# The expert blocks' down product as three fp32r products of split operands, with the weight's low part made on GpSimd

## What is computed

```python
shared = jax.nn.silu(flat @ sg) * (flat @ su) @ sd
probs = jax.nn.softmax(flat @ router_w, axis=-1)
topk_p, topk_i = jax.lax.top_k(probs, K_TOP)            # K_TOP = 2, 8 experts
topk_p = topk_p / (jnp.sum(topk_p, axis=-1, keepdims=True) + 1e-09)
cw = jnp.zeros((N, E)).at[jnp.arange(N)[:, None], topk_i].add(topk_p)
h = jax.nn.silu(jnp.einsum('nd,edf->nef', flat, wg)) * jnp.einsum('nd,edf->nef', flat, wu)
eo = jnp.einsum('nef,efd->ned', h, wd)
routed = jnp.einsum('ned,ne->nd', eo, cw)
return (shared + routed).reshape(B, T, D)
```

## Time and profile before

| | |
|---|---|
| three runs | 1410.91 us median, 1410.36 to 1414.53 |
| the profiled execution | 1408.87 us, its span 1407.1 us |
| TensorE busy | 97% of the span |
| VectorE, ScalarE, GpSimd busy | 61%, 56%, 59% of the span |
| granted TensorE clock | 1.00 throughout |
| expert blocks, gate product 0 to 14 | 1245.03 to 1381.54 us |

### The profile page before, as it was taken

The page is one execution under the profiler, slowest core; times in us unless marked ns, Lnnn a source line. Parts: engine busy times, 40 slices in busy tenths (PEclk is TensorE's granted clock), DMA queues, the critical chain, the costliest instruction groups (busy, mean ns, idle before and its releaser), DMA issues. The chain is left out here.

```text
span 1407.1 us, 23293 instructions
## 1 busy us (share of the span) xinstructions
PE 1371.2 (97%) x8766; PEld 1121.1 (80%) x8766; DVE 853.3 (61%) x1424; ACT 794.8 (56%) x1235; POOL 833.8 (59%) x721
## 2 busy tenths in 40 slices
PE   5999999999999999999999999999999899989998
PEld 3678888888888888888888888888888567766664
DVE  5565565566556556665655666565555657657564
ACT  3455666666566666656666665666655613245652
POOL 3466777777677777767777776777766434210002
PEclk9999999999999999999999999999999999999999
DMA  7577666766766676766666766766687645279994
GB/s 283 168 121 138 108 126 107 133 118 132 127 123 123 110 132 115 132 128 125 108 126 116 130 116 137 133 107 119 101 178 140 159 151 215 82 302 364 365 366 136
DMA packets 115231, 218.10 MB, mean 155 GB/s; under 512 B 13360, under 2 KB 49200, under 8 KB 108976
## 3 DMA queue, kind: packets, MB, share of 16 engines
q1 hardware_dynamic: 111968, 209.00, 66.2%
q0 software_dynamic: 1280, 4.20, 0.9%
q10 hardware_dynamic: 1872, 3.41, 0.6%
HBM read 132.67 MB, written 16.78 MB: 106 GB/s over the span
## 5 line engine op out<-in xcount | busy, mean ns | idle before, releaser
L587 POOL TENSOR_TENSOR p_parts<-probs,p_parts 128x512 fp32r<-128x512 f32 x256 | 340.2, 1348 | 248.5 <-ACT p_parts L644 248.5
L644 ACT ACTIVATE p_parts<-probs 128x512 fp32r<-128x512 f32 x256 | 147.7, 625 | 237.8 <-PE banks L962 237.8
L769 DVE TENSOR_TENSOR probs<-banks,probs 128x1024 f32<-128x1024 f32 x128 | 156.7, 1224 | 145.7 <-ACT probs L650 145.7
L674 ACT ACTIVATE probs<-probs 128x1024 f32<-128x1024 f32 x128 | 135.9, 1062 | 140.0 <-POOL probs L594 139.9
L911 PE MATMUL banks<-wv_hi,x_hi 128*128 128x512 f32 x512 | 206.7, 404 | 0.0
L929 PE MATMUL banks<-x_hi,wk_hi 128*128 128x512 f32 x512 | 201.7, 394 | 0.0
L912 PE MATMUL banks<-wv_lo,x_hi 128*128 128x512 f32 x512 | 201.1, 393 | 0.0
L913 PE MATMUL banks<-wv_hi,x_lo 128*128 128x512 f32 x512 | 200.1, 391 | 0.0
L931 PE MATMUL banks<-x_hi,wk_lo 128*128 128x512 f32 x512 | 199.6, 390 | 0.0
L930 PE MATMUL banks<-x_lo,wk_hi 128*128 128x512 f32 x512 | 199.3, 389 | 0.0
L958 PE MATMUL banks<-p_parts,v_hi 128*65 128x128 f32 x1024 | 191.7, 224 | 0.0
(11 more groups left out here) (305 smaller groups left out, 2679.5 us busy)
## 6 DMA issues: line engine op xcount, KB each, us to landing
queries<-q_scratch SPq DMA_DIRECT2D x256, 128.0 KB, 6.5
keys<-wo_room SPq DMA_DIRECT2D x128, 256.0 KB, 5.6
keys<-turned_odd SPq DMA_DIRECT2D x128, 256.0 KB, 5.6
row_room<-in_ctx SPq DMA_DIRECT2D x64, 256.0 KB, 6.4
wo_room<-in_down SPq DMA_DIRECT2D x10, 1024.0 KB, 9.1
late_room<-in_gate SPq DMA_DIRECT2D x8, 1024.0 KB, 8.1
gate_raw<-in_up SPq DMA_DIRECT2D x8, 1024.0 KB, 7.2
up_raw<-in_gate SPq DMA_DIRECT2D x7, 1024.0 KB, 7.9
```

The costliest lines, as they stand in the source:

```text
L587: nc.gpsimd.tensor_tensor(p_parts[:, 1, j, :], probs[:, pair % 2, j, :], p_parts[:, 0, j, :].bitcast(F32), ALU.subtract).then_inc(p_lo_rea ...
L769: nc.vector.tensor_tensor(mine, ps_s[:, :, :, 0, :].rearrange("p j i n -> p (j i) n"), mine, ALU.add).then_inc(s_taken, 1)
```

## The change

- The down product becomes `product` on split operands: 12 fp32r matmuls. Its operands are `ht_hi` (ScalarE, in the place of `ht`), `ht_lo` (VectorE, `hidden_low`), `down_hi` (ScalarE, `down_high(j)` behind silu j) and `down_lo` (GpSimd, a subtraction of 128x2048 behind the scatters, one a block).
- The split down weights lie in the buffers of the shared expert's operands, xt_hi, xt_lo, h_hi and h_lo, so the gathers now land in raw[1] and raw[2].
- A down buffer is free when its low part is made, no longer after its product. Down loads 1 and 2 are issued in `mix`'s last stretch, behind a wait for its out products.
- `rank_tokens` comes ahead of up product 1 of the shared expert, not in its middle; `find_places` comes ahead of the first `h_lo`; `split_low(2)` behind `find_owners`.
- The transposes of rows 0 stand in front of the last quarter of the shared down product, and VectorE takes the low part of rows 0 ahead of the shared additions. The transposes of hidden 0 come behind gate product 1, not between its matmuls.
- `late_shares` is one batch in each of blocks 3 to 6, and the shares are transposed and copied in block 8, not 5.
- VectorE counts its steps with one semaphore in all stages.

```diff
@@ run_sp
                 if j >= 3:
-                    sp.wait_ge(e_down_done, j - 2)
+                    sp.wait_ge(down_lo_ready, j - 2)
                 sp.dma_start(down[j % 3], d["down"][expert]).then_inc(down_landed[j % 3], 16)
...
             load_unit(unit_of(0, UP), 1)
             load_unit(unit_of(1, GATE), 2)
+            sp.wait_ge(keep["out_done"], BATCH)
+            load_down(1, 2)
+            load_down(2, 3)
             load_unit(unit_of(1, UP), 2)
             sp.wait_ge(scattered, 16 * 2 * BATCH)
...
             load_rows(2)
-            load_down(1, 2)
             load_unit(unit_of(2, UP), 3)
@@ run_pool
                     nc.gpsimd.indirect_dma_start(d["row_scratch"], bass.IndirectOffsetOnAxis(pos[:, k, b:b + 1], 0),
                                                  x_norm[:, b, :], None).then_inc(scattered, 16)
+            for m in range(BLOCKS):
+                pool.wait_ge(down_hi_ready, m + 1)
+                nc.gpsimd.tensor_tensor(down_lo[m % 2], down[m % 3], down_hi[m % 2].bitcast(F32), ALU.subtract).then_inc(down_lo_ready, 1)
             for i in range(2):
                 pool.wait_ge(e_stored[i], 16 * ((BLOCKS - LATE + 1 - i) // 2))
@@ run_act
+            def down_high(m):
+                act.wait_ge(down_landed[m % 3], 16 * (m // 3 + 1))
+                if m == 0:
+                    act.wait_ge(gate_up_done, KT)
+                elif m == 1:
+                    act.wait_ge(shared_done, BATCH)
+                else:
+                    act.wait_ge(e_down_done, m - 1)
+                nc.scalar.activation(down_hi[m % 2], down[m % 3], ACT.Copy).then_inc(down_hi_ready, 1)
...
-                    nc.scalar.activation(ht[:, (j - 1) % 2], ps_turn, ACT.Copy).then_inc(ht_ready, 1)
+                    nc.scalar.activation(ht_hi[:, (j - 1) % 2], ps_turn, ACT.Copy).then_inc(ht_hi_ready, 1)
...
                     nc.scalar.activation(silu[:, j % 2, :], ps_gate[:, 0, :], ACT.Silu).then_inc(e_silu_ready, 1)
+                    down_high(j)
@@ run_dve
+            def hidden_low(m):
+                dve.wait_ge(ht_hi_ready, m + 1)
+                if m >= 2:
+                    dve.wait_ge(e_down_done, m - 1)
+                nc.vector.tensor_tensor(ht_lo[:, m % 2], ps_turn, ht_hi[:, m % 2].bitcast(F32), ALU.subtract).then_inc(ht_lo_ready, 1)
...
             choose()
-            split_low(2)
             for f in range(KT):
...
+                if f == 0:
+                    find_places()
                 dve.wait_ge(h_hi_ready, f + 1)
...
                 if f == 0:
-                    find_places()
                     find_owners()
+                    split_low(2)
...
             split_low(4)
+            rows_low(0)
             for b in range(BATCH):
                 dve.wait_ge(shared_done, b + 1)
                 nc.vector.tensor_tensor(y[:, b, :], ps_y[:, b, :], x3[:, b, :], ALU.add).then_inc(y_added, 1)
-            rows_low(0)
...
                 if j == 0:
                     rows_low(1)
+                else:
+                    hidden_low(j - 1)
...
-                if j == 3:
-                    late_shares()
+                if 3 <= j < 3 + BATCH:
+                    late_shares(j - 3)
+            hidden_low(BLOCKS - 1)
@@ run_pe
-            gate_or_up(1, UP, whole, range(KT // 2))
             rank_tokens()
-            gate_or_up(1, UP, whole, range(KT // 2, KT)).then_inc(gate_up_done, 1)
+            gate_or_up(1, UP, whole, range(KT)).then_inc(gate_up_done, 1)
...
                 pe.wait_ge(h_lo_ready, t + 1)
+                if t == KT - 1:
+                    pe.wait_ge(rows_landed[0], 16)
+                    for i in range(KT):
+                        tr = turn(ps_rows, rows[:, 0, :], i)
+                    tr.then_inc(rows_turned, 1)
...
+                if j == 1:
+                    pe.wait_ge(e_hidden_ready, 1)
+                    for t in range(KT):
+                        tr = turn(ps_turn, hidden[:, 0, :], t)
...
-                    pe.wait_ge(ht_ready, m + 1)
-                    pe.wait_ge(down_landed[m % 3], 16 * (m // 3 + 1))
+                    pe.wait_ge(ht_lo_ready, m + 1)
+                    pe.wait_ge(down_lo_ready, m + 1)
...
-                        mm = nc.tensor.matmul(ps_y[:, m % 2, :], ht[:, m % 2, t, :], down[m % 3][:, t, :],
-                                              start=(t == 0), stop=(t == KT - 1))
+                        mm = product(ps_y[:, m % 2, :], (ht_hi[:, m % 2, t, :], ht_lo[:, m % 2, t, :]),
+                                     (down_hi[m % 2][:, t, :], down_lo[m % 2][:, t, :]), t == 0, t == KT - 1)
```

More of the change, by code:

```diff
@@ L201, in prepare @@
         ones_ready = sem("a_ones_ready")
-        dve_step = sem("a_dve_step")
+        dve_step = keep["dve_step"]
         var_ready = sem("a_var_ready")
@@ L301, in run_dve @@
         def run_dve(dve):
-            chain = [0]
+            chain = keep["dve_steps"]
             def link(ins):
@@ L1103, in mix @@
         attn_turned, attn_t_ready, wo_done = (keep[n] for n in ("attn_turned", "attn_t_ready", "wo_done"))
-        dve_step = sem("c_dve_step")
+        dve_step = keep["dve_step"]
         var_ready = sem("c_var_ready")
@@ L1119, in mix @@
         out_done = sem("c_out_done")
+        keep["out_done"] = out_done
         out_t_ready = sem("c_out_t_ready")
@@ L1420, in experts @@
         rt_lo = sb("rt_lo", [P, 2, KT, P], F32R)
-        ht = sb("ht", [P, 2, KT, P])
+        ht_hi = sb("ht_hi", [P, 2, KT, P], F32R)
+        ht_lo = sb("ht_lo", [P, 2, KT, P], F32R)
+        down_hi, down_lo = [xt_hi[:], h_hi], [xt_lo[:], h_lo]
         by_token = x_norm[:, 0:2, :].rearrange("p a (b n) -> p (a b) n", n=LATE * P)
@@ L1456, in experts @@
         ps_logits = ps_y[:, 3, 0:BATCH * EXPERTS].rearrange("p (b e) -> p b e", e=EXPERTS)
-        gathered = [h_hi.bitcast(F32), h_lo.bitcast(F32)]
+        gathered = [raw[1], raw[2]]
         raw_landed, split_hi, split_lo = keep["split_landed"], keep["split_hi"], keep["split_lo"]
@@ L1469, in experts @@
         route_counted = sem("route_counted")
-        router_step = sem("router_step")
+        dve_step = keep["dve_step"]
         pos_ready = sem("pos_ready")
@@ L1482, in experts @@
         h_turned = sem("h_turned")
-        ht_ready = sem("ht_ready")
+        ht_hi_ready = sem("ht_hi_ready")
+        ht_lo_ready = sem("ht_lo_ready")
+        down_hi_ready = sem("down_hi_ready")
+        down_lo_ready = sem("down_lo_ready")
         e_down_done = sem("e_down_done")
@@ L1540, in run_sp @@
                     load_unit(unit_of(j, UP), expert_of[j])
-                load_down(j - 1, expert_of[j - 1])
+                if j > 3:
+                    load_down(j - 1, expert_of[j - 1])
             for b in range(BATCH):
@@ L1625, in run_dve @@
         def run_dve(dve):
-            chain = [0]
+            chain = keep["dve_steps"]
             def link(ins):
                 chain[0] += 1
-                ins.then_inc(router_step, 1)
-                dve.wait_ge(router_step, chain[0])
+                ins.then_inc(dve_step, 1)
+                dve.wait_ge(dve_step, chain[0])
             def per_token(a):
@@ L1869, in take_late @@
                         mm.then_inc(late_done, 1)
-            pe.wait_ge(rows_landed[0], 16)
-            for t in range(KT):
-                tr = turn(ps_rows, rows[:, 0, :], t)
-            tr.then_inc(rows_turned, 1)
             for j in range(BLOCKS + 1):
@@ L1882, in run_pe @@
                     pe.wait_ge(split_lo, v + 1)
[L1883 removed]
+                if j >= 2:
                     pe.wait_ge(e_hidden_ready, j)
[L1885 to L1886 removed]
+                    pe.wait_ge(ht_lo_ready, j - 1)
                 for t in range(KT):
@@ L1915, in run_pe @@
                     m = j - 1
-                    if j == 5:
+                    if j == 8:
                         turn_shares()
@@ L1963, in program @@
         keep["attn_t"] = room
+        keep["dve_step"], keep["dve_steps"] = sem("dve_step"), [0]
         keep["angles_landed"] = [sem(f"angles_landed{i}") for i in range(2)]
```

31 lines of the change are left out of this document (14 added, 17 removed).

## The result

The changed kernel took 1413.73 us (median of 20 runs, 1409.76 to 1416.98), the kernel before 1409.61 beside it (20 runs, 1407.79 to 1415.06). The ratio is 1.0019 with a 95% interval of 1.0010 to 1.0028, so 2.7 us more (1.4 to 3.9). The two medians by themselves lie 4.1 us apart; I go by the ratio, which has the interval. The prediction was 1413.3 us, and +2.4 for the change.

The account below looks back on a forecast made before the run. It took TensorE's matmuls to set the pace in the blocks. Start -2.2, gate 0 to 2 +1.6, gate 2 to 14 -2.4 and tail +5.4 sum to +2.4 us: 1413.3 from the median 1410.91, range 1406 to 1419.

Parts of the forecast that it names:

- GpSimd's subtraction: In each expert block, GpSimd's 128x2048 subtraction for the down weight's low part takes 4.5 us.
- The two engines keep each other out: In the blocks, VectorE's two-operand split of the up weight stands until GpSimd's subtraction finishes, showing 3.4 to 4.5 us.
- Rival B: In the blocks, the engines hardly block each other, so waits of 7.7 us go: 1405.6 us; chance 0.15.
- A wait in every second block: At the up product, the low weight comes 0.8 us late in every second block, 0.4 a block.
- down 2.4: From gate product 2 to gate product 14, the stretch falls from 119.7 to 117.3 us.
- Share blocks: In blocks 3 to 6, VectorE's share work makes ht_lo late: 0.8 us each, 0.4 more in block 3, 3.6 in all.
- Gate 0 to 2: From gate product 0 to 2, TensorE waits 0.5 and 2.3 us, so the stretch grows 1.6 to 18.4.
- The start: Before gate product 0, earlier places and scatters bring it forward 2.2 us, with a 0.3 wait for the rows.
- The tail: After gate product 14, the gathers queue behind GpSimd's fifteenth subtraction: 31.0 us for 25.6, up 5.4.
- rival C: After gate product 14, the gathers don't set the end; tail 24.3 to 27 us, total 1407 to 1409; chance 0.07.
- Rival D: In the blocks, transfers need 9.56 us against 9.2 and the slack doesn't hold: 1415 to 1416 us; chance 0.06.
- Rival A: In the blocks, GpSimd's subtraction takes 5.4 us, mean wait 0.85 a block and more: 1420 us; chance 0.22.

Follow-up runs that it names:

- e3: Changed kernel with each GpSimd subtraction of 128x2048 cut into four of 128x512; 1413.17 us, ratio 1.0018 to the kernel before.
- e5: Changed kernel with GpSimd computing only the first two down low parts, which later blocks reuse; 1399.46 us, ratio 0.9922 to the kernel before.
- e6: Changed kernel with the share work spread over blocks 1 to 12, its transposes in block 13; 1412.95 us, ratio 1.0018 to the kernel before.
- e4: Changed kernel with the old order of the start; 1415.91 us, ratio 1.0034 to the kernel before.
- e10: Kernel before the change with only the new order of the start; 1409.14 us, ratio 0.9984 to the kernel before.
- e1: Changed kernel with the fifteenth down weight's low part on VectorE instead of GpSimd; 1405.91 us, ratio 0.9966 to the kernel before.
- e9: Changed kernel, all down low parts on VectorE ahead of the up split, one small share operation in each of blocks 0 to 13; 1397.39 us, ratio 0.9914.
- e12: Changed kernel with GpSimd computing the first quarter of each down low part once more; 1428.53 us, ratio 1.0127 to the kernel before.
- e11: Changed kernel with the down loads of blocks 1 and 2 at their old queue places; 1412.07 us, ratio 1.0009 to the kernel before.

## Why the prediction was right, point by point

The mechanisms were right: the two engines that keep each other out, the waits at the places named, and the queue in the tail. That the sum of the stages hit so closely (+2.33 for +2.4) is luck: the start gave 0.7 us more than worked out and the blocks 0.8 less, and these cancelled. So is part of the match in the total: 1413.3 was added up from a median of 1410.91 for the kernel before, which then measured 1409.61.

- **The down product** (2.85, measured 2.88; a block without waits 9.2, measured 9.23): right. The 0.03 in twelve blocks is 0.4 us.
- **GpSimd's subtraction** (4.5): 4.63. The line through its 512 and 1024 rows was the right estimate, the average of the attention stage the wrong one.
- **The two engines keep each other out:** shown by e3 and e5. Rival B is out, although its price was about right between gate 2 and gate 14: without its 2.3 for block 1 its 7.7 us leave 5.4 there, and e5 gained 6.1.
- **A wait in every second block** (0.8): 0.90, of which the rows give 0.62 as idle; three of them add 0.3 us. With the transposes at 1.04 for 0.95 and the 0.4 above, this is the 0.8 by which "down 2.4" missed (-1.62).
- **Share blocks** (3.6): the four intervals from gate 4 to gate 8 exceed 9.23 by 3.57. The size was right, its naming was in part not: by e6 1.9 of it stand there without the share work too, and moving this work away nets only 1 us.
- **Gate 0 to 2** (+1.6): +1.63, with waits of 0.46 and 2.14 for the 0.5 and 2.3 predicted.
- **The start** (-2.2): -2.88, the largest miss. The eight scatters took 12.3 us from the first's start to the last's end, for 13.3 before (two of them, issued while splits of VectorE's ran, took 2.00 and 2.17 us for the usual 0.96; before, 2.71 and 1.89), so the wait of 0.3 for the rows did not come, and gate 0 started 0.65 earlier than worked out. e4 and e10 show it by themselves.
- **The tail** (+5.4): +5.20. e1 shows that it is all the queue behind GpSimd's last subtraction, so rival C is out. It decides the sign: without it the change is 0.34% faster.
- **Rival D** is out: e5 and e9 run blocks of 9.2 to 9.3 us at a transfer share of 1.01, and none of ScalarE's copies waits for a load.
- **Rival A's price was too low**, by "mean wait 0.85 a block": e12 pays 14.8 us for 1.38. In proportion (an estimate from e12's two numbers), 5.4 us for the subtraction would have meant 8 us over the changed kernel, near 1422, beyond my range. This step would have failed had the case come.
- **The early loads** (nothing): e11 agrees.

## What to carry to other kernels

Work that is moved to an empty engine is not free when that engine shares a lock with a busy one, and when other instructions queue behind it there: look for both, here GpSimd with VectorE's two-operand subtractions and with the gathers. VectorE with all the work (19.25 of 20 us), in the right order and with the share work spread (e9), beat VectorE helped by GpSimd by 1.05%, 15 us by the two ratios; some 6 of them are the tail's. Before giving work away, look at what stands ahead of each idle stretch of the engine, and fill it.

## What the runs showed of the hardware beside that

The granted clock falls behind short waits in some executions and not in others of the same code. The stretch 1205:1210 (columns as in the earlier trace rows), in the kernel before:

```profile
1205.00:1210.00 5.00, 5.00 (x37) 3.96 (x36) 0.69 (x1) 0.68 (x2) 0.00 (x0) 1.00 0.00 0
```

and in the changed one, where nothing in it differs:

```profile
1205.00:1210.00 5.00, 4.76 (x27) 4.76 (x28) 2.07 (x4) 1.07 (x2) 0.00 (x0) 0.66 0.04 16
```

TensorE had waited 1.50 and 0.40 us ahead of it in both, and here it fell to the lower level (1.2 GHz) for a while. One load's issue on SyncE's queue, shortly ahead, before and after:

```profile
1191.55 0.35 SPq L1505 DMA_DIRECT2D up_raw<-in_gate  x1
```

```profile
1192.98 0.34 SPq L1511 DMA_DIRECT2D up_raw<-in_gate  x1
```

So 1.43 us of the 2.77 by which the two traces differ ahead of the experts arise ahead of 1190, and 1.34 behind it, with this fall. The changed kernel's trace has one more fall, near 1097 (0.66 in 1095:1100, 1.00 before), but it doesn't explain the 1.43: the changed kernel's ScalarE is 1.7 us behind already at 1068, and 1.4 behind at 1108. In the blocks the same 2.1 us wait ahead of up product 1 left the clock alone in the changed kernel, e4, e5 and e6, and lowered it in e1 and e11:

```profile
1255.00:1260.00 5.00, 4.85 (x17) 3.65 (x17) 2.90 (x3) 0.94 (x1) 3.98 (x1) 0.66 0.78 290
```

That is e1, where gate 0 to gate 2 took 19.98 us for 18.42. Such a fall costs 1.3 to 1.6 us (1.34 above, 19.98 and 20.01 for 18.42 here), more than half of what this change did, so stages were compared here and not spans. Each of these six traces has one of the two falls and not the other: the changed kernel, e4, e5 and e6 the one near 1205, e1 and e11 the one in block 1. What decides between the two cases is open.
